# Twelve small layers on one core: the cross attention's loop in another order, value tiles kept from the first layer, quantised weights unpacked one layer early, and fewer, fuller tiles in one expert layer

## The reference, cut to what matters

```python
q = (x @ Wq.T + bq); k = (ctx @ Wk.T + bk); v = (ctx @ Wv.T + bv)      # 16 heads of 16 channels
out = softmax(q k^T / 4 + mask) v @ Wo.T + bo                           # L3x: without biases
```

```python
w1 = (fc1_q - 128) * scales1;  y = silu(layernorm(x) @ w1 + b1)         # 256 -> 1024
w2 = (fc2_q - 128) * scales2;  out = x + 0.5 * (y @ w2 + b2)            # 1024 -> 256
```

## Time and profile before

| | us |
|---|---|
| median of the runs shown (1659.79 to 1663.58) | 1661.11 |
| the profiled execution's own time | 1664.46 |
| its span, first to last instruction | 1662.7 |
| TensorE busy | 1544.9 |
| VectorE busy | 1028.4 |
| ScalarE busy | 918.0 |

### The profile page before, as it was taken

The page is one execution under the profiler, slowest core; times in us unless marked ns, Lnnn a source line. Parts: engine busy times, 40 slices in busy tenths (PEclk is TensorE's granted clock), DMA queues, the critical chain, the costliest instruction groups (busy, mean ns, idle before and its releaser), DMA issues.

```text
span 1662.7 us, 34203 instructions
## 1 busy us (share of the span) xinstructions
PE 1544.9 (93%) x14044; PEld 1147.0 (69%) x14044; DVE 1028.4 (62%) x1933; ACT 918.0 (55%) x1371; POOL 9.7 (1%) x22
## 2 busy tenths in 40 slices
PE   6999998988999999999987998899999999997897
PEld 5777587756677777777766675677777777775663
DVE  5522323656777787777775325677777777777631
ACT  3021032127777777777774222677777777778610
POOL 0000000000000000000000000000000000000000
PEclk9999999899999999999999999999999999999999
DMA  9667854245434243434322364543424243324445
GB/s 394 221 199 237 312 193 197 80 171 186 153 142 169 90 169 110 149 112 168 115 87 109 129 244 166 179 155 118 156 89 156 90 156 108 139 89 166 161 170 206
DMA packets 39533, 267.67 MB, mean 161 GB/s; under 512 B 4760, under 2 KB 5016, under 8 KB 32152
## 3 DMA queue, kind: packets, MB, share of 16 engines
q1 hardware_dynamic: 39384, 265.55, 44.0%
HBM read 159.49 MB, written 3.28 MB: 98 GB/s over the span
## 4 chain that ended last, share of the span: by engine, by line
PE 77%; ACT 7%; DMA 6%; DVE 5%; issue 3%; SPq 1%; POOL 0%; DVEq 0%; ACTq 0%; POOLq 0%
PE T L786 14%; PE O L808 8%; PE S L772 8%; PE O L786 7%; PE T L744 7%; PE T L757 5%; PE S L648 4%; ACT sc L1199 4%; PE O L744 3%; PE O L942 3%; PE T L643 3%; PE S L1094 3%; PE O L1123 3%; PE O L757 2%; DMA keys<-keys_hl 2%
## 5 line engine op out<-in xcount | busy, mean ns | idle before, releaser
L1612 DVE CUSTOM_DVE_ANT_0 sc<-S,mask_bias,small 128x896 f32<-128x896 f32 x336 | 377.7, 1149 | 62.7 <-PE S L772 56.7
L1199 ACT ACTIVATE sc<-sc,small 128x1792 f32<-128x1792 f32 x168 | 299.8, 1786 | 2.3 <-DVE small L1612 1.0
L1185 ACT ACTIVATE pT<-T 128x512 f32<-128x512 f32 x378 | 220.2, 594 | 123.1 <-PE T L786 119.4
L786 PE MATMUL T<-consts,sc 128*128 128x128 f32 x1592 | 239.6, 281 | 6.8 <-ACT sc L1199 2.2
L786 PEld LDWEIGHTS T<-consts,sc 128*128 128x128 f32 x1592 | 176.1, 141 | 72.9 <-issue 38.2
L808 PE MATMUL O<-pT,arena 128*32 128x128 f32 x6272 | 198.4, 278 | 28.8 <-ACT pT L1185 28.8
L808 PEld LDWEIGHTS O<-pT,arena 128*32 128x32 f32 x6272 | 169.4, 111 | 67.9 <-issue 66.6
L772 PE MATMUL S<-keys,q 64*128 64x512 f32 (+1 forms) x896 | 150.8, 414 | 15.5 <-DVE small L1612 14.3
L1578 DVE COPY pT<-T 128x512 f32<-128x512 f32 x150 | 99.9, 686 | 100.1 <-PE T L786 100.0
L1185 ACT ACTIVATE pT<-O 128x512 f32<-128x512 f32 x182 | 108.1, 594 | 56.0 <-PE O L786 54.9
L1612 DVE CUSTOM_DVE_ANT_0 packs<-S,mask_bias,small 128x896 f32<-128x896 f32 x112 | 128.5, 1147 | 0.0
(11 more groups left out here) (355 smaller groups left out, 1905.8 us busy)
## 6 DMA issues: line engine op xcount, KB each, us to landing
keys<-keys_hl SPq DMA_DIRECT2D x112, 896.0 KB, 7.9
ctx_in<-in_ctx_cols SPq DMA_DIRECT2D x46, 896.0 KB, 7.0
wide<-in_ctx_rows SPq DMA_DIRECT2D x14, 896.0 KB, 4.7
wide<-in_up_L0f SPq DMA_DIRECT2D x8, 1408.0 KB, 9.7
sc<-in_ctx_cols SPq DMA_DIRECT2D x10, 896.0 KB, 5.7
wide<-in_up_L2f SPq DMA_DIRECT2D x8, 1024.0 KB, 6.6
wide<-in_down_L2f SPq DMA_DIRECT2D x8, 1024.0 KB, 4.9
wide<-in_up_L3f SPq DMA_DIRECT2D x4, 2048.0 KB, 9.0
```

Of the source, the lines that this page charges most:

```text
L786: last = nc.tensor.transpose(ring(plan, u)[:, t * P:(t + 1) * P], weights_of(2 * m + i)[:, b * P:(b + 1) * P], ident)
L1185: nc.scalar.activation(pT2[:, g * BANK:(g + 1) * BANK], ring(plan, u), ACT.Copy).then_inc(s["t_act"], 1)
L1199: nc.scalar.activation(weights_of(n), weights_of(n), ACT.Exp, bias=n_best[c % 2][:, h:h + 1], scale=-1.0, accum_out=l_new[c % 2][:, h:h + ...
L1612: V.tensor_tensor_reduce(weights_of(n)[:, i * HC:(i + 1) * HC], S4f[:, n % 2 * 2 * BANK:n % 2 * 2 * BANK + HC], mask_bias[:, i * HC:(i + 1 ...
```

## The change

1. **Loop of `cross`.** Scores half 0 follow group 0, a value unit follows group 2, groups 3 to 5 stay together, and one key unit stands ahead of `multiply` in every pair (`KEY_STEPS`; value units by `VALUE_STEPS`). VectorE takes groups 0 and 4, ScalarE 1, 2, 3, 5, 6 and the value units. The quad and the second head's scores change places on VectorE.
2. **Key copies in halves of the tokens**: `load_keys(c, hf, half)`, each with a semaphore of its own, 16 DMAs per chunk instead of 8; waits for keys follow.
3. **Value units kept.** `KEPT["L2x"]` is 2, 0, 2, 2, 7, 2, 2 by chunk: the five other units of chunk 4 are made in L0a (`after`), from the chunk's data that lie in `sc`, in place of dummy matmuls. 17 units instead of 12 are stored, by two DMAs, which wait for `after_taken`.
4. **L0f's tiles.** Six tiles of 128 rows (the last 64) instead of eight of 88: six transposes, six down products, a down DMA of 128 rows of 6 KB. L2f's eight tiles of 128 stay.
5. **L1a and L1f.** Each weight matrix is unpacked by one `scalar_tensor_tensor`, the first while L1a waits for `num_ps`, the second behind `oT`. In L1f the early value units move ahead of the transposes they followed, the first product is made and softened in halves, and ScalarE takes the second half of `yT`.
6. **Residuals.** Biases are added ahead of the wait for the last product (L0x, L0a, L1x, L1f, L2x).
7. **L3f.** SP issues up 4, 5, up 6, 7, then down 4, 5, down 6, 7; 14 dummy matmuls instead of 20 ahead of `pos`.

```diff
-KEPT = {"L2x": 2, "L3x": 0}
-PROJECTED = {
-    "L2x": {0: [("V", 2)], 1: [("K", 0, 0), ("V", 3)], 2: [("K", 0, 1), ("K", 0, 2)], 3: [("K", 0, 3), ("V", 4)],
-            4: [("V", 5)], 5: [("K", 1, 0), ("V", 6)], 6: [("K", 1, 1), ("K", 1, 2)], 7: [("K", 1, 3)]},
...
+WHOLE = 4
+KEPT = {"L2x": [0 if c == 1 else 7 if c == WHOLE else 2 for c in range(7)], "L3x": [0] * 7}
+KEY_STEPS = [(hf, nb) for hf in range(KD) for nb in range(KEY_UNITS)]
+VALUE_STEPS = {"L2x": {0: 2, 2: 3, 3: 4, 4: 5, 6: 6}, "L3x": {j: j for j in range(VALUE_UNITS)}}
...
-    return "act" if u[0] == "T" and u[2] not in (0, 1) else "dve"
+    return "act" if u[0] == "V" or u[0] == "T" and u[2] not in (0, 4) else "dve"
...
-                    def load_keys(c, hf):
+                    def load_keys(c, hf, half):
...
                         for r in range(KEY_COPIES):
-                            sp.dma_start(keys4[r::KEY_COPIES, hf * HH // 2:(hf + 1) * HH // 2, :].bitcast(F32),
-                                         keys_hl[:, r % 2, :].bitcast(F32)).then_inc(s[f"keys_in{hf}"], 16)
+                            sp.dma_start(keys4[r::KEY_COPIES, hf * HH // 2:(hf + 1) * HH // 2, part].bitcast(F32),
+                                         keys_hl[:, r % 2, part].bitcast(F32)).then_inc(s[f"keys_in{hf}{half}"], 16)
...
-                        load_keys(c, 0)
+                        load_keys(c, 0, 0)
+                        load_keys(c, 0, 1)
                         load_next_ctx(c, 0)
-                        load_keys(c, 1)
+                        load_keys(c, 1, 0)
                         load_next_ctx(c, 1)
+                        load_keys(c, 1, 1)
...
                 for m in range(PAIRS):
-                    for g in range(3):
-                        turn(m, g)
+                    turn(m, 0)
                     if m + 1 < PAIRS:
                         scores(m + 1, 0)
-                    turn(m, 3)
-                    project(m, 0)
-                    turn(m, 4)
-                    turn(m, 5)
+                    turn(m, 1)
+                    turn(m, 2)
+                    if plan.values_of(m):
+                        value_unit(*plan.values_of(m)[1:])
+                    for g in range(3, 6):
+                        turn(m, g)
                     if m + 1 < PAIRS:
                         scores(m + 1, 1)
                     turn(m, TURNS - 1)
                     if quad_turned(m) is not None:
                         turn_quad(quad_turned(m))
-                    project(m, 1)
+                    if plan.keys_of(m):
+                        key_unit(*plan.keys_of(m)[1:])
                     multiply(m)
...
-                    qkv(layer, x2T, 25)
+                    qkv(layer, x2T, 1)
...
+                if layer == "L0a":
+                    after(2, T2[:, 1])
+                    after(3, O2[:, 1])
+                    after(4, S4[:, 3], 2)
...
-                    sp.wait_ge(s["held_taken"], len(HELD))
-                    sp.dma_start(held_out, held).then_inc(s["held_out"], 16)
+                    sp.wait_ge(s["held_taken"], len(PASSING))
+                    sp.wait_ge(s["after_taken"], len(AFTER))
+                    sp.dma_start(held_out[:, 0:IN_ARENA], held_a).then_inc(s["held_out"], 16)
+                    sp.dma_start(held_out[:, IN_ARENA:len(HELD)], held_b).then_inc(s["held_out"], 16)
...
-                    for t in range(E):
-                        last = mm(O2[:, b, 0:D], hidT[0:F // E, t, :], w[:, t, :], start=(t == 0), stop=(t == E - 1))
+                    for t, rows in tiles(layer):
+                        last = mm(O2[:, b, 0:D], hidT[0:rows, t, :], w[0:rows, t, :], start=(t == 0),
+                                  stop=(t == tiles(layer)[-1][0]))
...
-                    for b, bank in ((4, T2[:, 0]), (5, T2[:, 1]), (6, O2[:, 1])):
-                        early("L2x", b, bank)
-                    warm(S4[:, 3], 8)
-                    need(pe, "dve", f"{layer}.w")
+                    need(pe, "dve", "L1a.w")
...
                     for i in range(2):
+                        warm(T2[:, 0], 8 * i)
+                        need(pe, "act", f"{layer}.y{i}")
+                        done("pe", transposes(S4[:, 2 + i], hid[:, i * BANK:(i + 1) * BANK], 4), f"{layer}.yT_ps{i}")
...
+            def unpack_weights(b):
+                return link(V.scalar_tensor_tensor(fb[:, b, 0:2048], fb[:, b, 0:2048].bitcast(I32), 128.0,
+                                                   fb[:, b, 2048:4096], ALU.subtract, ALU.mult))
```

More of the change, by code:

```diff
@@ L46, with tiles @@
 GATED = ("L0f", "L3f")
+def tiles(layer):
+    return [(f // P, min(P, FF[layer] - f)) for f in range(0, FF[layer], P)]
 PACKS = {
@@ L668, in early, with after @@
                 last.then_inc(s["early_ready"], 1)
+            def after(n, bank, free=0):
+                s = L["L0x"]
+                if n == 0:
+                    pe.wait_ge(s["held_taken"], len(PASSING))
+                if free:
+                    pe.wait_ge(s["after_taken"], free)
+                b = AFTER[n][1]
+                chunk = sc[:, 0:2, :].rearrange("p h (k n) -> p h k n", k=KD)
+                for t in (2 * b, 2 * b + 1):
+                    part, at = divmod(t, TB // 2)
+                    for k in range(KD):
+                        last = mm(bank[:, (t % 2) * D:(t % 2 + 1) * D], chunk[:, part, k, at * P:(at + 1) * P],
+                                  early_wv[:, k, :], start=(k == 0), stop=(k == KD - 1))
+                last.then_inc(s["after_ready"], 1)
             def norm(layer):
@@ L677, in norm @@
                     early("L3x", 6, T2[:, 1])
+                    warm(T2[:, 0], 3)
+                elif layer == "L1f":
+                    early("L2x", 4, T2[:, 1])
                     warm(T2[:, 0], 3)
@@ L684, in norm2 @@
             def norm2(layer):
-                warm(T2[:, 1], 13)
+                if layer == "L0a":
+                    after(1, S4[:, 3])
+                    warm(T2[:, 1], 5)
+                elif layer == "L1f":
+                    early("L2x", 5, O2[:, 1])
+                    early("L2x", 6, S4[:, 3])
+                    pe.wait_ge(L["L2x"]["early_taken"], 5)
+                else:
+                    warm(T2[:, 1], 13)
                 need(pe, "dve", f"{layer}.x2")
@@ L957, in expert @@
                     for j in range(2):
-                        last = transposes(T2[:, j], hid[:, j * F // 2:(j + 1) * F // 2], 4, F // E)
+                        for t, rows in tiles(layer)[4 * j:4 * j + 4]:
+                            last = nc.tensor.transpose(T2[0:rows, j, t % 4 * P:(t % 4 + 1) * P],
+                                                       hid[:, t * P:t * P + rows], ident)
                         last.then_inc(s["t_ready"], 1)
@@ L1220, in cross @@
                     key_unit(0, 0, nb)
+                for b in plan.values:
+                    value_unit(0, b)
                 for n in range(2):
@@ L1235, in cross @@
                         take_quad(quad_turned(m))
-                    take_turned(m, 3)
-                    project(m, 0)
-                    for g in range(4, TURNS):
+                    if plan.values_of(m):
+                        value_unit(*plan.values_of(m)[1:])
+                    for g in (3, 5, 6):
                         take_turned(m, g)
@@ L1677, in cross @@
                 done("dve", V.scalar_tensor_tensor(q4f, qT, C["part"][:, 1:2], q_up, ALU.mult, ALU.add), f"{layer}.q4")
-                for b in plan.values:
-                    value_unit(0, b)
                 take_mask(0)
@@ L1760, in _ @@
                     take_held(NC - 1)
-                    need(dve, "pe", f"{layer}.out")
-                    residual(layer, O2[:, 0, 0:D])
+                    packed(dve, layer)
+                    residual(layer, "out", O2[:, 0, 0:D])
                 elif layer == "L0a":
@@ L1981, in _ @@
                     done("dve", V.tensor_copy(arena[:, 1024:1024 + 768], S4f[:, 0:768]), f"{layer}.fT")
-                    need(dve, "pe", f"{layer}.out")
-                    residual(layer, O2[:, 1, 0:D])
+                    residual(layer, "out", O2[:, 1, 0:D])
 def blocks(w):
@@ L2057, in layout @@
             [i[n].reshape(E, F, KD, P).transpose(0, 3, 2, 1).reshape(E, P, KD * F) for n in names], axis=2)
-        out[f"down_{layer}"] = i[downs[layer]].reshape(E, D, E, F // E).transpose(0, 3, 2, 1).reshape(E, F // E, E * D)
+        n = len(tiles(layer))
+        down = np.zeros((E, n * P, D), np.float32)
+        down[:, 0:F] = i[downs[layer]].reshape(E, D, F).transpose(0, 2, 1)
+        out[f"down_{layer}"] = down.reshape(E, n, P, D).transpose(0, 2, 1, 3).reshape(E, P, n * D)
     return {k: np.ascontiguousarray(v) for k, v in out.items()}
```

254 lines of the change are left out of this document (141 added, 113 removed), and 3 rows, old and new, of the table PROJECTED.

## The result

The median fell from 1662.34 us (1659.79 to 1664.24, 4 runs) to 1591.53 us (1588.98 to 1594.11, 4 runs): a ratio of 0.9575, 95% interval 0.9554 to 0.9596. By the medians that is 70.8 us. The profiled execution took 1588.98 us, the fastest of its four, 75.5 less than the 1664.46 of before.

What follows compares the result with a forecast made beforehand. It took TensorE's work and the chain of waits inside single pairs to bound the kernel. Terms summed to -71.6 us, giving 1592.9 from the profiled execution, 1589.5 from the median; forecast 1590, 8 in 10 range 1572 to 1620.

Steps and rivals of the forecast that it cites:

- L2x, -26: L2x's loop: chunk 0 -9.5, full chunks -1 together, chunk 3 -8.5, last chunk -6, first scores -1; together -26 us.
- L3x, -15: L3x's loop: chunk 0 -11, chunks 1 to 5 nothing, last chunk -4 because of L3a's decays on ScalarE; together -15 us.
- The chain I had drawn for pairs with a key: Each cross pair: a ring of waits through scores, exponentials and group 0, 7.4 us, against 7.92 of TensorE work.
- Key copies, 0: Key copies in halves: needed at least 22 us after issue, so costed at nothing.
- L0f, -11: L0f: an expert falls from 9.05 to 7.96 us and stalls on up weights go; -11, or -7 at the old landing time.
- L1f, -10: L1f: first product starts at once behind `x2T`, then 10.3 us to the end; -10 us.
- L1a, +0.2: L1a: unpacking costs 0.2 us behind `oT`, otherwise no extra time.
- L0a, +0.5: L0a: value units replace dummies and the store goes out later, near 58.3; up to 0.5 us lost.
- L3f, -8.6: L3f: the 5.34 us wait for up weights goes, lower TensorE level worth 2.6, six fewer dummies 0.7; together -8.6 us.
- Biases, -1.7: Biases added ahead of waits: one instruction of 0.42 us saved in four layers, -1.7 us.
- ScalarE late in each pair: Rival, cross loop: group 5 waits for ScalarE's value copy, 0.2 to 0.5 us per pair, 1612 to 1646; chance 0.2.
- The floor: Rival, cross loop: mask and summing are hidden after all, -12 us, 1578; chance 0.12.

Runs made afterwards that it cites:

- full_tile_ups_first: New kernel, with L0f's down product taking its last tile with all 128 rows and the next up weights issued ahead of the down product's wait: 1587.18 us.
- before_96_rows: Kernel before, with L0f's down weights padded by zero rows from 88 to 96 in the load only: 1664.33 us, ratio to before 1.0003.
- before_scores_first: Kernel before, with TensorE doing the next pair's first scores behind group 0 instead of group 2: 1683.42 us, ratio to before 1.0144.
- values_at_seven: New kernel, with value units in pairs 1, 3, 4, 5, 7 of L2x's chunks and all but pair 3 of L3x's: 1583.22 us.
- all_together: New kernel with moved value units, L0f's full last tile with up weights first, five dummies for eight between L1f's halves: 1578.26 us.

## Why the prediction was right, and where its terms were off

The time was right, 1590 for 1591.53. The sum was -71.6, the medians fell by 70.8 and the profiled executions by 75.5. The large terms were in the right places, but that the sum comes within 1 us of the medians is partly luck: L0f gave less than its term, the full chunks gave more. And of the 46.7 us by which the two cross attentions fell between the profiles, 7.7 are TensorE at a lower clock in the execution of before: 2.8 in L3x's fill, 1.5 in the slow pair of L2x's last chunk, and about 1.1 and 2.3 in the second pairs of L2x and L3x, 11.08 us at a granted clock of 0.89 and 12.23 at 0.79 for 9.97 at full clock later in the chunk.

- **L2x, -26; it was -30.4.** Chunk 0: the last of its eight periods already holds a value unit of chunk 2's (10.09 for 8.41), and without it the chunk takes 66.3, forecast 66. Chunk 3, likewise less one unit, 67.0 (forecast 67.5). The last chunk 7.45 a pair (7.5), -6.4 (-6), of which 1.5 is the slow pair. What was mis-sized are the full chunks, 75.3 where I said 75.8: the mask and the summing cost 0.72 and 0.64, not 0.95 each. The first product with the values came 1.5 us sooner, not 1 (38.47 to 36.96 us into the layer); I gave this to the halves of the key copies, but with both halves issued late it is still 36.95, so its cause is open.
- **L3x, -15; it was -16.3.** Chunk 0 gave 10.9 (11), full chunks 0.2 each. The fill, 42.7 to 40.0, is no gain of the code: the new kernel's fill takes 42.73 in `full_tile_ups_first`, where the granted clock over it is the same 0.92 as before, and 39.96 where it is 1.00. Without these 2.8 L3x gave 13.5, less than its term. The last chunk gave 1.6, not 4: the decays for L3a, 1.26 us of ScalarE in each of four pairs, hold three of them at 8.34; the first two take 8.86 and 9.64. I named them and took too little. The fill of before and that of `full_tile_ups_first`, in the columns of the earlier trace rows, the granted clock third from the end:

```profile
999.33:1042.07 42.74, 36.16 (x146) 23.44 (x147) 25.80 (x45) 11.84 (x19) 0.55 (x1) 0.92 0.52 185
950.59:993.32 42.73, 37.74 (x150) 24.14 (x151) 21.83 (x38) 16.68 (x26) 0.55 (x1) 0.92 0.59 201
```

- **Why the loop gained.** Undoing the scores' place costs 36.6 us by the medians, undoing group 1's engine 49.6, nearly all of it in the two layers, and moving the scores alone makes the old kernel slower. Place and engine are one edit. Kept units are 8.4 of the gain, half copies 3.0, value copies 5.0; these don't add up. With the scores in their old place a kept unit is worth 0.87 us a pair (9.70 for 8.83), not 1.68 (9.65 for 7.97), for the pairs without it are held by VectorE: chunks 2 and 3 take 75.90 and 73.41 there for the 76.80 of a full one, 4.3 less together. Without kept units that run would have L2x at 558.4, as an estimate; before it was 560.6, 559.1 without the slow pair's 1.5. So the new distribution of keys alone would be hardly better than the old one.
- **The chain of a pair.** The chain I had drawn for pairs with a key was the wrong one. It doesn't go through the exponentials; it is TensorE's own work plus VectorE's two scores, which need 2.3 to 2.4 us, and what counts is that TensorE's work between the halves is as long (five groups, 2.4) while a key unit covers the copy of group 6 (0.78). In its pairs with one unit the old order had a unit for the first of these only, in the last chunk for neither; its pairs with two units had both, and those without a quad took 9.65 to 9.8, as pairs with a value do now. So it is not so that a unit between groups 3 and 4 lengthened the ring instead of filling it; it filled it, and the wait for group 6 was left. No run moves the key unit alone, so its share was read, not tested.
- **Key copies, 0; they gave 3.0.** The term looked at when copied keys are read, not at when their source is overwritten. The estimate beside it has a slip: with a fixed part of 2 us, half a copy lands 1 us later than half the time of a whole one, not 2; measured is 0.5 (4.5 against half of 7.9).
- **L0f, -11; it was -8.5.** An expert took 8.33 us, later up to 8.7, not 7.96. The missing term is the change from 128 rows to 64 and back, 0.35 an expert (8.33 - 7.98), 2.8 in eight; with it gone and SP's order mended, 7.98. That the stalls go was right, and `before_96_rows` speaks for the number of rows as the reason. The transfers moved 280 GB/s at a share of 0.71, some 394 at a full one, where I said 425.
- **L1f, -10; it was -9.4**, from `x2T` on 10.35 us for 10.3 (the terms listed add up to 10.2). The start came later: the value unit ahead of it took 3.03 us, others of the layer 1.89. **L1a, +0.2; it was +0.9**, and L1a reads between 39.2 and 41.2 in the runs here, 40.1 and 41.0 with the old kernel's code, so nothing here tells the unpacking's part.
- **L0a, +0.5; it was -2.0.** The store at 58.02 (58.3 forecast) and no weights late. The old code takes 31.51 at a granted clock of 0.91, 30.05 in `before_scores_first` at 1.00; the new one 29.48 at 1.00. So 1.5 of the 2.0 are the clock, 0.6 the code. **L3f, -8.6; it was -8.9**, and undoing the loads' order gave 8.0 back.
- **Biases, -1.7.** The term holds for L0a, L1x, L1f and L2x: from the end of the last product to the next layer's first statistics are 0.57 us in the first three where there were 0.95, and in L2x the addition stands ahead of the wait. In L0x it still comes last, behind the copies of the value units. L2f is 0.4 shorter too, but it has no such bias; there VectorE's wait for GpSimd ahead of the last scaling is 0.51 us where it was 0.89, for a reason that isn't known.

Of the rivals, ScalarE late in each pair would have shown in pairs of more than 8.1: they take 7.97. The floor isn't reached, as `values_at_seven` shows by lowering it. None of the rivals named what the gain hangs on: with VectorE's order one copy off, the gain of the loop is gone.

## What to carry to other kernels

Where two halves of a step share a buffer, look at how much of the bounding engine's work lies between them, and at what the other engine has to do before it may start on the first half; an early issue without an early start is a loss. When an engine gets faster, read the wait that then ends last: in L0f the time taken from the down product came back as a wait for weights until SP issued in the order in which buffers come free. Place filler work in the steps where another engine is late, not evenly. And before a layer's difference between two profiles is put down to an edit, compare the granted clock over it: here L3x's fill shrank by 2.8 us and the code had no part in it.

## What the runs showed of the hardware

Changing the number of rows of the stationary tile from 128 to 64 and back costs TensorE 0.3 us in a series of twelve products (2.88 against 2.59); 64 rows of zeros are cheaper than the change.

Zero rows that make a DMA's rows 96 instead of 88 let the next load land in 8.2 us instead of 9.5.

The same layer differs by up to 3.7 us between executions, with the same code, and goes with the granted clock. L0a reads 29.48 in four of the profiled executions, all at 1.00, and up to 31.99 in others, at 0.88; L2a 23.9 to 27.6; L3a 11.84, 13.15 or 14.8; the new kernel's fill of L3x 39.96, 41.65 or 42.73, at 1.00, 0.96 and 0.92. The dummies ahead of L0f's first transposes, first in `full_tile_ups_first`, where the granted clock over them is 0.55, then in `all_together`, whose code is the same there, at 1.00:

```profile
74.16 4.58 PE L686 MATMUL T<-consts 128*128 128x128 f32 x22
```

```profile
71.68 2.62 PE L686 MATMUL T<-consts 128*128 128x128 f32 x22
```

Mostly at the lower of TensorE's two levels, 1.2 GHz, the dummies outlast the wait that they fill, and the first product with the up weights comes 5.08 us into the layer; at 2.4 GHz it comes at 3.45. In the kernel before, runs of 1659.29 and 1668.10 us had mean granted clocks of 0.988 and 0.983. These steps are larger than several of the terms above, so terms under 2 us in the short layers can be told only where two executions have the same granted clock; a pair of the cross attention repeats to 0.02 us as long as its clock is full.
